# The queries for the relative keys: one projection, a trip through DRAM and 128 small loads, in place of eight masked products a tile

## The reference, cut to what matters

```python
q = split_heads(x @ Wq + bq)                       # (b, 16, 512, 8)
scores = jnp.einsum('bhid,bhjd->bhij', q, k)
rel = jnp.einsum('bhid,pd->bhip', q, rel_key)      # (b, 16, 512, 256)
rel_idx = jnp.clip(j - i + p - 1, 0, p - 1)
bias = jnp.take_along_axis(rel, broadcast(rel_idx), axis=3)
logits = jnp.where(j <= i, (scores + bias) * scale, -inf)
attn = softmax(logits);  out = einsum('bhij,bhjd->bhid', attn, v)
```

## Time and profile before

| | before |
|---|---|
| median of three executions | 947.34 us |
| the profiled execution: time | 946.77 us |
| its span on the core | 944.7 us |
| PE busy | 764.6 us, 81% |
| ACT busy | 495.8 us, 52% |
| DVE busy | 449.9 us, 48% |
| POOL busy | 178.9 us, 19% |

### The profile page before, as it was taken

The page is one execution under the profiler, slowest core; times in us unless marked ns, Lnnn a source line. Parts: engine busy times, 40 slices in busy tenths (PEclk is TensorE's granted clock), DMA queues, the critical chain, the costliest instruction groups (busy, mean ns, idle before and its releaser), DMA issues.

```text
span 944.7 us, 21455 instructions
## 1 busy us (share of the span) xinstructions
PE 764.6 (81%) x8384; PEld 548.1 (58%) x8384; DVE 449.9 (48%) x1528; ACT 495.8 (52%) x1013; POOL 178.9 (19%) x306
## 2 busy tenths in 40 slices
PE   1677888798987899988999987678786787489994
PEld 0466777576765576675565753255553563267773
DVE  3154543665545364435345552474765535521416
ACT  0335555457754659765658753548554554233321
POOL 4200101000010000010000003033324382115411
PEclk9999999899997999998999998989998998879998
DMA  3500110001300001200000410110411120011011
GB/s 99 178 2 2 68 61 2 1 3 45 114 2 12 1 13 48 89 25 12 2 13 2 130 31 20 44 29 26 154 46 45 42 61 23 6 29 46 23 34 37
DMA packets 36440, 38.29 MB, mean 41 GB/s; under 512 B 8982, under 2 KB 26220, under 8 KB 36212
## 3 DMA queue, kind: packets, MB, share of 16 engines
q1 hardware_dynamic: 34548, 33.65, 11.8%
q0 software_dynamic: 1536, 3.15, 1.1%
q10 hardware_dynamic: 256, 0.13, 0.0%
HBM read 19.87 MB, written 16.91 MB: 39 GB/s over the span
## 4 chain that ended last, share of the span: by engine, by line
PE 54%; DVE 17%; issue 14%; ACT 10%; ACTq 1%; another core or an unknown queue 1%; DMA 1%; POOL 1%; SPq 1%; POOLq 0%; DVEq 0%
PE ps L1696 5%; PE ps L1545 5%; PE ps L1566 4%; PE ps L1711 4%; PE ps L1771 4%; PE ps L1473 3%; PE ps L1579 3%; PE ps L1548 3%; PE ps L1783 3%; ACT late L908 3%; ACT probsT L758 3%; PE ps L1542 2%; PE ps L1646 2%; PE ps L1794 2%; DVE stats L1017 2%
## 5 line engine op out<-in xcount | busy, mean ns | idle before, releaser
L908 ACT ACTIVATE late<-ps,j_bias 128x512 f32<-128x512 f32 x256 | 174.7, 694 | 152.6 <-PE ps L1696 131.3
L1171 DVE TENSOR_REDUCE neg_max<-ps 128x2 f32<-128x32 f32 (+31 forms) x128 | 90.5, 707 | 166.7 <-PE ps L1551 161.5
L1696 PE MATMUL ps<-q_heads,k_parts 128*128 128x512 f32 x256 | 135.1, 542 | 20.4 <-ACT late L908 17.6
L758 ACT ACTIVATE probsT<-ps 128x128 f32<-128x128 f32 (+3 forms) x256 | 98.1, 438 | 81.0 <-PE ps L1566 67.3
L834 ACT ACTIVATE probs<-ps,neg_max 128x16 f32<-128x16 f32 (+31 forms) x256 | 110.5, 495 | 32.2 <-DVE neg_max L1171 32.2
L627 POOL TENSOR_TENSOR q_wide<-qT,eighth_mask 128x1024 f32<-128x1024 f32 x16 | 31.2, 1950 | 368.4 <-PE ps L1551 285.7
L1566 PE MATMUL ps<-ident,probs 128*128 128x128 f32 x640 | 95.6, 280 | 2.1 <-ACT probs L834 2.1
L1696 PEld LDWEIGHTS ps<-q_heads,k_parts 128*128 128x128 f32 x256 | 49.8, 200 | 72.3 <-ACT late L908 47.5
L1545 PE MATMUL ps<-kT_two,q_wide 64*64 64x262 f32 (+16 forms) x1024 | 72.7, 347 | 15.8 <-ACT probsT L758 10.3
L1566 PEld LDWEIGHTS ps<-ident,probs 128*128 128x128 f32 x640 | 74.9, 142 | 18.2 <-issue 8.2
L1711 PE MATMUL ps<-late,v_two 128*9 128x512 f32 x512 | 73.0, 636 | 9.5 <-DVE late L1157 8.3
(11 more groups left out here) (265 smaller groups left out, 1245.7 us busy)
## 6 DMA issues: line engine op xcount, KB each, us to landing
k_parts<-k_half SPq DMA_DIRECT2D x16, 256.0 KB, 3.3
q_parts<-q_half SPq DMA_DIRECT2D x16, 256.0 KB, 3.5
k_parts<-k_parts SPq DMA_DIRECT2D x16, 256.0 KB, 3.1
q_heads<-q_parts SPq DMA_DIRECT2D x64, 64.0 KB, 2.1
x_by_expert<-q_heads SPq DMA_DIRECT2D x3, 960.0 KB, 7.6
probsT<-x_by_expert SPq DMA_DIRECT2D x45, 64.0 KB
y_by_expert<-probsT SPq DMA_DIRECT2D x45, 64.0 KB
late<-in_L_ffn_w_dram SPq DMA_DIRECT2D x1, 2048.0 KB
```

Of the source, the lines that this page charges most:

```text
L758: return nc.scalar.activation(o, i, ACT.Copy)
L908: nc.scalar.activation(head_probs[:, i % SLOTS, :], ps[:, banks[i % len(banks)], :], ACT.Exp, bias=j_bias[:]).then_inc(e2_ready.sem, 1)
L1171: nc.vector.tensor_reduce(neg_max[:, n % 4, :], ps[:, k:k + OCT, 0:QS * (n + 1)], axis=AXX, op=ALU.max, negate=True).then_inc(max_ready.se ...
L1696: mm(ps[:, banks[i % R], :], k_parts[:, hg, kc * P:(kc + 1) * P], q_heads[:, hg % 2, g, :], start=True, stop=True).then_inc(s2_ready.sem, 1)
```

## The change

- `relative` on PE and DVE, with `wq_rep`, is gone. `head` gets one more pair of pieces: PE projects the queries of all four tiles with tokens on the partitions (`by_distance`, four products of 128 columns), DVE scales them and adds the bias into `q_nat` in one instruction, and SP writes them to DRAM (256 KB).
- `q_rel` is zeroed once by POOL. For each tile SP reads the eight places i back by eight DMAs into the partitions i, i+8, ...; each moves 256 runs of 8 numbers (32 bytes).
- For the runs to be whole, partitions of `q_rel` and `toep` are now (octet, feature, place) and columns of `q_wide`, `q_rel` and `ahead_pick` are (token, head), before (head, token). `toep` is written by 8 DMAs of 16 partitions, before 16 of 8, and the sine comes after the fourth.
- The turned probabilities then lie in PSUM as (token, head). `probsT` keeps head before token, so the copy writes neighbours of PSUM 64 numbers (256 bytes) apart, before in runs of eight.
- In `plan` the R pieces of PE and DVE vanish; R is one piece a tile for SP and POOL, H begins at slot 45, before 50.
- On SP the loads of `w1`, `w2` and the second attention's weights, before at the start, come after the first tiles' loads of `q_rel`, and PE waits for both `w1` and `w2` before it turns the first.

```diff
         for r in range(B + 2):
             if a < B:
-                put(r, 0, "R", a, 4)
+                put(r, 0, "R", a, 1)
+                put(r, 14, "R", a, 1)
+                put(r, 30, "R", a, 1)
...
-                put(r, 13 + late, "R", a, 4)
...
-                put(r, 34 + late, "R", a, 4)
...
-                put(r, 50, "H", a + 1, 10)
-                put(r, 60, "R", a + 1, 4)
+                put(r, 45, "H", a + 1, 12)
+                put(r, 52, "R", a + 1, 1)
             put(r, 52, "S", f, 1)
...
-        yield from [("H", 0)] * 10 + [("R", 0)] * 4
+        yield from [("H", 0)] * 6 + [("R", 0)] + [("H", 0)] * 6
...
-        q_wide = sb("q_wide", [P, 2, BPT, HO, QB])
-        q_rel = sb("q_rel", [P, 2, BPT, HO, QB])
+        q_wide = sb("q_wide", [P, 2, BPT, QB, HO])
+        q_rel = sb("q_rel", [P, 2, BPT, QB, HO])
...
+            def head(b):                                   # SP
+                for _ in range(5):
+                    yield
+                sp.wait_ge(b7_free, fill_no["H", b, 4] + 1)
+                sp.dma_start(q_nat_dram[b].rearrange("t n i e c -> (n i) t (e c)"), q_nat[:]).then_inc(q_nat_out.sem, 16)
+                yield
+
+            def relative(b):                               # SP
+                if b == 0:
+                    sp.wait_ge(q_rel_zero, 1)
+                sp.wait_ge(q_nat_out.sem, q_nat_out.at(b + 1, 0))
+                for t in range(T):
+                    if b * T + t >= 2:
+                        sp.wait_ge(scores_ready.sem, scores_ready.at(b, SPT * (t - 1)))
+                    for i in range(QB):
+                        sp.dma_start(q_rel[i:P:QB, t % 2, :, i, :],
+                                     q_nat_dram[b][t, :, i, :, :].rearrange("n e c -> e n c")).then_inc(q_rel_in[t % 2], 16)
+                    yield
...
-            copy(probsT[:, 0:c, o, :, (n % SPT) * QB:(n % SPT + 1) * QB],
-                 ps[:, turned_bank(b, n, o), 0:c * P].rearrange("p (c r i) -> p c r i", r=2 * HO, i=QB)
+            copy(probsT[:, o, 0:c, :, (n % SPT) * QB:(n % SPT + 1) * QB].rearrange("p c (z h) i -> p (c z) i h", z=2),
+                 ps[:, turned_bank(b, n, o), 0:c * P].rearrange("p (k i h) -> p k i h", i=QB, h=HO)
                  ).then_inc(done.sem, 1)
...
-            for r in range(0, P, RR):
-                for i in range(QB):
-                    c = S - QB - NREL + 1 + i
-                    rows = slice(r + i * D, r + (i + 1) * D)
-                    act.dma_start(toep[rows, c:c + NREL], rel_rows[rows, :]).then_inc(toep_dma, 16)
-            act.wait_ge(j_ready, 1)
-            nc.scalar.activation(j_turn, j_row, ACT.Sin, accum_out=j_sum[:]).then_inc(j_ready, 1)
-            nc.scalar.preload_act_table_set("exp_and_others")
+            for i in range(QB):
+                if i == QB // 2:
+                    act.wait_ge(j_ready, 1)
+                    nc.scalar.activation(j_turn, j_row, ACT.Sin, accum_out=j_sum[:]).then_inc(j_ready, 1)
+                    nc.scalar.preload_act_table_set("exp_and_others")
+                c = S - QB - NREL + 1 + i
+                act.dma_start(toep[i:P:QB, c:c + NREL], rel_rows[i:P:QB, :]).then_inc(toep_dma, 16)
...
-            def relative(b):                               # DVE
-                for t in range(T):
-                    for half in range(2):
-                        yield
-                        full("R", b, 4 * t + 2 * half)
...
-                        for j in range(4):
-                            c = 4 * half + j
-                            last = nc.vector.scalar_tensor_tensor(
-                                out=q_rel[:, t % 2, :, c, :],
...
-                        last.then_inc(b7_free, 1)
-                        yield
+                full("H", b, 4)                            # DVE, in head
+                if b:
+                    dve.wait_ge(q_nat_out.sem, q_nat_out.at(b, 0))
+                nc.vector.scalar_tensor_tensor(
+                    out=q_nat[:], in0=token_tiles(B7), scalar=SCALE, op0=ALU.mult, op1=ALU.add,
+                    in1=q_bias_nat[:].rearrange("p o d c -> p (o d c)").unsqueeze(1).broadcast_to([P, T, P])
+                    ).then_inc(b7_free, 1)
...
+                by_distance = w_qkvo[:, 0, :].rearrange("e (o c d) -> e o d c", o=OCT, d=D)
+                for t in range(T):                         # PE, in head
+                    last = mm(bank7[:, t * P:(t + 1) * P], head_T[:, t * P:(t + 1) * P], by_distance,
+                              start=True, stop=True)
...
-            def relative(b):                               # PE
-                for t in range(T):
-                    for half in range(2):
-                        fill("R", b, 4 * t + 2 * half)
-                        for j in range(4):
-                            last = mm(bank7[:, j * P:(j + 1) * P], wq_rep[:, 4 * half + j, :, :, :],
-                                      head_T[:, t * P:(t + 1) * P], start=True, stop=True)
...
+                    if (kind, a) == ("w1", 0):             # PE, in weights
+                        pe.wait_ge(ld_experts, 2 * 16)
...
             def scores(b, n):
...
-                    pe.wait_ge(b7_free, fill_no["R", b, 4 * t + 2] + 1)
+                    pe.wait_ge(q_rel_in[t % 2], 16 * QB * (b * T // 2 + t // 2 + 1))
```

More of the change, by code:

```diff
@@ L308, in build_sandwich @@
                           for n in "kq"]
+        q_nat_dram = [nc.dram_tensor(f"q_by_token_{b}", [T, BPT, QB, OCT * D, HO], f32, kind="Internal").ap()
+                      for b in range(B)]
         x_dram = [nc.dram_tensor(f"x_by_expert_{b}", [ROWS, P], f32, kind="Internal").ap() for b in range(LAST)]
@@ L342, in build_sandwich @@
         ld_bias = sem("ld_bias")
+        ld_experts = sem("ld_experts")
+        q_rel_zero = sem("q_rel_zero")
+        q_rel_in = [sem(f"q_rel_in{k}") for k in range(2)]
         toep_dma = sem("toep_dma")
@@ new lines, in weights @@
+            def weights(b):
+                sp.dma_start(w1_in, w1.rearrange("(m p) e d -> p m e d", p=P)).then_inc(ld_experts, 16)
+                sp.dma_start(w2_in[:], w2).then_inc(ld_experts, 16)
+                for m, w in enumerate(MATS):
+                    for c in range(4):
+                        rows = slice(c * QD, (c + 1) * QD)
+                        for p0, n, by in ([(0, 4, 1)], [(0, 2, 2), (1, 2, 2)], [(0, 2, 1), (2, 2, 1)],
+                                          [(i, 1, 1) for i in range(4)])[c]:
+                            w0 = c ^ p0
+                            sp.dma_start(w_quat[rows, m, p0:p0 + (n - 1) * by + 1:by, :],
+                                         w[w0:w0 + (n - 1) * by + 1:by].rearrange("w d o -> d w o")
+                                         ).then_inc(ld_quat, 16)
+                for _ in range(45):
+                    yield
+                sp.wait_ge(heads_zero, 1)
+                for b in range(LAST):
+                    sp.dma_start(x_dram[b].rearrange("(p n) d -> p (n d)", p=P),
+                                 q_heads[:].rearrange("p a g s -> p (a g s)")[:, 0:ROWS].bitcast(f32)
+                                 ).then_inc(rows_zero, 16)
+                yield
@@ L571, in all_experts @@
                 yield
-            take({"S": spread, "Q": quat, "X": by_expert, "C": sums, "D": all_experts})
+            take({"H": head, "R": relative, "W": weights, "S": spread, "Q": quat, "X": by_expert, "C": sums,
+                  "D": all_experts})
             sp.wait_ge(x_stored.sem, x_stored.at(B, 0))
@@ L792, in head @@
                 yield
-                full("H", b, 4)
+                yield
+                yield
+                full("H", b, 6)
                 if b >= 1:
@@ L798, in head @@
                 yield
-                full("H", b, 6)
+                full("H", b, 8)
                 nc.scalar.activation(kT_two[:, b % 2, :], bank7, ACT.Identity, bias=k_bias[:])
@@ L804, in head @@
                 yield
-                full("H", b, 8)
+                full("H", b, 10)
                 if b == 0:
@@ L1406, in all_experts @@
                 yield
-            take({"H": head, "R": relative, "W": weights, "A": attention, "F": ffn, "Q": quat, "N": norm,
+            take({"H": head, "W": weights, "A": attention, "F": ffn, "Q": quat, "N": norm,
                   "X": by_expert, "C": sums, "D": all_experts})
@@ L1547, in scores @@
                 for (rows, o, z), bank in zip(tiles, out_of):
-                    mm(bank[:, nears[z]:ends[z]], q_rel[rows, t % 2, blocks[z], :, :],
+                    mm(bank[:, nears[z]:ends[z]],
+                       q_rel[rows, t % 2, blocks[z], :, :],
                        toep[rows, S - ends[z] + nears[z]:S], start=False, stop=False, skip_group_check=True)
```

101 lines of the change are left out of this document (39 added, 62 removed).

## The result

The changed kernel takes 977.99 us (median of 4 runs, 975.36 to 985.36) against 946.4 us of the kernel before beside it: a ratio of 1.034, 95% interval 1.028 to 1.041. It is 32 us slower, where 922 us and 909 to 956 were forecast. The profiled execution has a span of 976.4 us.

The account below looks back on a forecast made before the run. PE was taken to bound the later rounds, a loop PE, DVE, ACT, PE round 0. Start -10.3, rounds -19, new projections +3.3, SP stalls +1 and copies unchanged gave -25, so 922 us, range 909 to 956.

Parts of the forecast that it names:

- I take the lower, the nearer shape: ACT's copies to `probsT`: writing 256 bytes apart costs nothing extra, 597 ns for 512 columns as before.
- The upper bound: ACT's copies to `probsT`: one more time per number, 0.84 ns, 68 us of ACT in all.
- The rival's price: Copies to `probsT` written at half the rate: +43 us, 966 us in all; chance 0.20.
- The chances: Forecast 0.45, copies pay 0.20, time hidden 0.18, dear loads 0.09, more 0.08; faster 0.80, lowered to 0.78.
- 1.1 us of TensorE for each new projection: Rounds: three more query projections by token, +3.3 us in all, DVE's instruction going beside.
- the first turn of `w1`: Start, PE: weights land at 48.7 us, so this comes 10.3 us earlier than 58.98.
- first scores: Start: begin at 33.1 us, 10.2 us earlier; 36.5 if an issue costs 0.9 us.
- The rounds: Attention behind the start: 0.65 of 29 us of removed products and masks comes back, -19 us.
- what stands against it: Rounds: three more projections by token, +3.3 us, and SP's stalls in rounds 1 and 2, +1.
- a load of `q_rel`: SP's small loads: 0.46 us each to issue, the last landing 1.9 us later.
- the wait for `w1`: Start: PE is ready at 44.2 us and waits 4.5 us for weights that land at 48.7.
- The stall on SP in round 1: Loads land at 261.8 us, needed at 261.3: 0.5 us; +1 with round 2, up to 5 with dear issues.

Follow-up runs that it names:

- e10: e1 with single 512-number instructions added behind its end to price jumps; ACT's copy took 0.60 us in a row, 1.07 when written every 4th.
- e1: Changed kernel with the copy's two inner loops exchanged: writes runs of eight, reads PSUM 32 bytes apart, same result; 937.5 us, ratio 0.992.
- e3: Kernel before with only the changed kernel's dear copy added (neighbours read, written 256 bytes apart); 977.6 us, ratio 1.034.
- e7: e1 with projections begun at even slot 48 in place of 45, R at 54 in place of 52; 917.5 us, ratio 0.976.
- e7b: Control to e7: e1 with projections begun at odd slot 47, R at 54; 927.3 us, ratio 0.988.
- e14: Changed kernel, dear copy and late weights kept, with only e7's slots (48 and 54); 956.8 us, ratio 1.021.
- e13_again: Second run of e11 plus four groups of useless products between the steps, none at the start; 910.0 us, ratio 0.970.
- e12_again: Second run of e11 plus 17 useless products in TensorE's idle time at the start, none between steps; 915.0 us, ratio 0.977.
- e8: e1 with the two 2 MB loads of w1 and w2 issued among the first loads again; 929.9 us, ratio 0.992.
- e11: e7 with e8's order of loads (w1 and w2 at the start); 920.9 us, ratio 0.972.

## Why the prediction was wrong

**The step that failed** is "I take the lower, the nearer shape" in the part on the copies. The upper bound was nearly right: 0.84 ns more per number forecast and 0.90 measured, 68 us of ACT forecast and 64 measured. The nearness was read wrongly: runs of eight 256 bytes apart and neighbours 256 bytes apart share the distance, but what counts is how many numbers are written together, and e10 shows that the distance doesn't count from 16 bytes on. The Trainium skill ("Advanced Engine Details and Errata", section Memory Cachelines) had said that: lines of 16 bytes, two hits on each or a penalty. It got a chance of 0.20 since no row showed it for ACT; the runs agree with it for ACT and DVE, reading and writing, and for TensorE's moving operand. What no row spoke against should not have been weighed down by an absence. The rival's price was nearly right as well: 43 us forecast, 40 (e1) and 32 (e3) measured. The chances as they stand add up to 0.82 for faster, where 0.80 is written; that decides nothing.

**The term that was missing**: where the projections stand in a step. The prediction used the new slots for SP's queue only and took 1.1 us of TensorE for each new projection as its whole cost, beside copies that nobody waits for. All four projections of a batch had moved from even to odd slots, ahead of the turns: 10 to 11 us (e7 against e7b), 12 in the kernel after (e14). The two orders of instructions, laid side by side at the end of a batch, show it without any run.

**The term that was missing at the start**: the first turn of `w1` came at 49.7 (48.7 forecast), but 9.3 us of lead there were 4.8 at step 12, since the rows kept the lower level for longer. Nearly as much is lost with cheap copies (11.9 us of lead at step 0 of e1, 5.2 at step 12), so the dear copies are not its cause. e13_again against e12_again prices what added products bring back at 5 us (0.6%), their own time already paid; the first group showed 0.1%.

With these, the sum: -25 as forecast, +40 for the copies, +12 for the slots, +5 for the clock make +32; 32 was measured. The terms come from several chips, and the 40 us hold some that the profiles place behind the attention, where these copies no longer run. That the sum meets the measured time to the us is luck. The runs show that the first two terms are of this order; the third rests on one group of runs out of two.

**Right:** `head_T` (18.5 us, 20.5 forecast) and first scores (31.75, 33.1). The rounds: e7, with cheap copies and even slots, gains 18.8 us from step 12 of batch 0 to the end of the attention (7.0 ahead, then 25.8); forecast were 19, less 3.3 and 1 for what stands against it, 14.7. In round 0 steps 12 to 24 took 41.9 us, 42.5 before, nothing gained, as the earlier trace rows had said. e7's ratio of 0.976 is 924 us, where the forecast said 922 and e7 still pays for the clock at the start.

**Mis-sized:** a load of `q_rel` took 0.65 us to issue (10.42 for 16), 0.46 taken, and lands in 2.4, 1.9 taken; the wait for `w1` 2.8 us, 4.5 taken. The stall on SP in round 1 is there in e1, 2.2 us, 0.5 taken. TensorE was to be busy 33 to 37 us less; it was busy 767.4 us, 2.8 more than before, and in e1 752.8. The 41.6 us are gone and 8.5 (L1474) came, 3 more than forecast, but the remaining rows grew longer: the products that the attention kept (L1562, L1565, L1584, L1597) took 299.1 us, before 280.9, and the stretch behind the attention 318.8, before 307.5. DVE was busy 31.2 us less, 33 forecast.

**Open:** behind the attention nothing changed, yet the kernel after took 408.9 us there and before 399.5; from 725 us on its granted clock reads 0.85, before 0.90 from 700 on. e14, with the same dear copies, has 0.88 and took 398.2 us there, and e3 402.2, so that the copies alone don't account for it. The four executions of the kernel after had a mean granted clock of 0.922 to 0.935, the six of e14 0.925 to 0.930. Whether that belongs to the kernel or to the execution wasn't tried.

## What to carry over

When a layout changes, look at each instruction that touches it and ask how many neighbours it reads or writes together in SBUF: from 16 bytes apart one alone costs up to twice the time (1.8 times on ACT, 1.5 on DVE for these copies), two are free, and a PSUM operand can take the jump in their stead. When pieces are moved in an order written by hand, look on which side of the turns, copies and exponentials of a step they come to stand, not only how far they move. A removed product can have been holding the clock up, and a slower copy can let it fall (e3); compare the duration of one shape over the first 70 us before trusting the gain at the start.

## What the hardware showed unexpectedly

- Every 2nd fp32 number of SBUF is as cheap as all (0.62 against 0.60 us for 512 on ACT), every 4th costs 1.07, every 8th 1.08; DVE has 0.69, 1.05, 1.07. TensorE's moving operand: 1.06 and 2.02 us for a pair of passes.
- ACT reads PSUM 32 bytes apart at full speed (0.60).
- TensorE's rows kept the lower level until 53 us in the kernel before, until 58 to 68 in the changed kernels; four groups of useless products between the steps, 5 to 6 us in all, ended that at 37 to 46. Seventeen such products ahead of the steps raised the level for some 2 us at most.
- With the dear copies in the kernel before (e3, one profile) the rows were short from 48.6 us and long again from 54 to 67.
- A DMA of 256 runs of 32 bytes is issued in 0.65 us and lands in 2.4. The 256 KB of `q_nat` let the first of them go 2.4 us after their own issue (e1 and after), and 4.5 to 6.5 us when 4 MB of weights were on the way (e8, e11).
